# First attention of a fused decoder block: scores as fp32 matmuls in 64x64 blocks, V whole, Y in 64x32 blocks, all engine orders laid anew

## What is computed

```python
q, k, v = split(x @ W_attn)                     # 16 heads of 8 channels
att = q @ k.T / sqrt(8); att = where(causal, att, -inf)
att = polymax(att)      # x*x+1 for x>0, 1-x/100 for -100<=x<=0, else 0; all /1000
x = layernorm(x + (att @ v) @ W_proj)           # first attention
x = layernorm(x + cross_attention(x, ctx, 16 heads of 64))   # softmax; second attention
x = layernorm(x + moe(x))   # 16 experts 128x128, gates from the top 6 of a softmax router
```

## Time and profile before

| | before |
|---|---|
| device time, median of 3 runs | 1042.84 us (1041.07 to 1043.26) |
| the profiled execution | 1043.48 us, its span 1041.4 us |
| PE / PEld busy | 993.9 / 868.0 us |
| DVE / ACT / POOL busy | 978.6 / 762.2 / 395.1 us |
| PE matmul instructions | 16856 |
| granted TensorE clock, mean | 0.986 |

### The profile page before, as it was taken

One profiled execution on the slowest core, in us unless ns is written; L12 is line 12 of the kernel. 1 busy time (PEld: TensorE's weight loads), 2 busy tenths in 40 slices (PEclk: granted clock), 3 DMA queues, 4 the chain that ended last, 5 costly groups with the idle time before them and its releaser, 6 DMA issues.

```text
span 1041.4 us, 44466 instructions
## 1 busy us (share of the span) xinstructions
PE 993.9 (95%) x16856; PEld 868.0 (83%) x16856; DVE 978.6 (94%) x3176; ACT 762.2 (73%) x1606; POOL 395.1 (38%) x681
## 2 busy tenths in 40 slices
PE   5999999999999999999999999999999999999974
PEld 4788888888888888888888888888888888888763
DVE  6779999999999999999999999999999999999766
ACT  5886787777778777778777777877777877776531
POOL 1432344433334434334443333444433444332331
PEclk9999999999999999999999999999999999999987
DMA  5100110000000000010000000000000000010000
GB/s 174 38 23 3 28 28 8 17 25 25 25 25 25 0 25 25 25 25 25 15 10 25 25 25 25 25 1 24 25 25 25 25 20 5 25 37 7 7 2 15
DMA packets 29577, 25.16 MB, mean 24 GB/s; under 512 B 2528, under 2 KB 24544, under 8 KB 29536
## 3 DMA queue, kind: packets, MB, share of 16 engines
q1 hardware_dynamic: 29536, 24.57, 8.5%
HBM read 20.37 MB, written 4.19 MB: 24 GB/s over the span
## 4 chain that ended last, share of the span: by engine, by line
DVE 39%; issue 26%; PE 24%; POOL 4%; ACT 4%; DVEq 2%; DMA 0%; ACTq 0%; POOLq 0%; SPq 0%
PE ps L420 22%; DVE sums L860 15%; DVE allowed L824 4%; DVE ps L831 3%; DVE stats L777 3%; DVE p L805 2%; ACT x L733 2%; POOL rstd L985 2%; DVE p L837 1%; DVE residual L860 1%; DVE left L896 1%; PE ps L571 1%; DVE mv L783 1%; PE ps L548 1%; DVE residual L945 1%
## 5 line engine op out<-in xcount | busy, mean ns | idle before, releaser
L860 DVE SCALAR_TENSOR_TENSOR sums<-ps,gate,sums 128x128 f32<-128x128 f32 x896 | 241.7, 345 | 1.5 <-ACT x L733 1.2
L992 POOL TENSOR_TENSOR p<-p,rowinv 128x1024 f32<-128x1024 f32 x64 | 121.9, 1904 | 36.0 <-DVE rowinv L813 36.0
L982 POOL TENSOR_TENSOR rstd<-mv,ln_eps_tile 128x2 f32<-128x2 f32 x96 | 18.7, 195 | 295.3 <-DVE mv L783 292.0
L420 PE MATMUL ps<-wo_sb,oT 128*128 128x128 f32 x1024 | 122.7, 278 | 2.9 <-issue 0.5
L420 PEld LDWEIGHTS ps<-wo_sb,oT 128*128 128x128 f32 x1024 | 116.7, 192 | 6.7 <-issue 6.2
L733 ACT ACTIVATE x<-residual,shift,rstd 128x128 f32<-128x128 f32 x192 | 83.9, 487 | 39.9 <-POOL shift L987 39.7
L420 PE MATMUL ps<-ex_hi,x2T_hi 128*128 128x512 f32 x256 | 106.7, 417 | 5.3 <-DVE p L805 2.7
L635 ACT ACTIVATE relu<-ps 128x512 f32<-128x512 f32 x128 | 75.9, 596 | 45.2 <-PE ps L420 44.5
L420 PE MATMUL ps<-ex_lo,x2T_hi 128*128 128x512 f32 x256 | 102.8, 402 | 0.0
L420 PE MATMUL ps<-ex_hi,x2T_lo 128*128 128x512 f32 x256 | 102.6, 401 | 0.0
L824 DVE SCALAR_TENSOR_TENSOR allowed<-ps,const 128x512 f32<-128x512 f32 x128 | 87.6, 686 | 8.5 <-ACT relu L635 5.7
(11 more groups left out here) (122 smaller groups left out, 2970.1 us busy)
## 6 DMA issues: line engine op xcount, KB each, us to landing
...
```

The lines of the kernel that those rows point to most:

```text
L420: return pe.matmul(o, l, r, start=start, stop=stop)
L860: done = V.scalar_tensor_tensor(after, ps(f"FF{4 * r + q}")[:, C * e:C * e + C], gate[:, r, 4 * q + e:4 * q + e + 1], before, ALU.mult, AL ...
L992: G.tensor_tensor(weights, weights, rowinv[:, r].unsqueeze(2).broadcast_to([P, H, T]), ALU.mult).then_inc(p2_ready, 1)
```

## The change

The first attention is written anew; the second attention, the experts and the norms keep their instructions.

- **Scores.** `s1` makes 8 fp32 matmuls per tile of 64x64 with N = 512, without a split: per call two sequences (columns of the array) by two halves of the channels (rows of the array). A score bank now holds partitions (sequence of the pair, key) and 512 columns = 8 heads x 64 queries. The keys are copied once whole (`kT`), the queries eight times on ACT, each masked to one head of a half (`qm`). `keys_lo` and `queries_lo` are gone from DVE.
- **V** is 2 matmuls of 128x128, N = 128, moved with one ACT instruction.
- **Y** is 64 matmuls of 64x32, N = 64: per row block, four heads after another accumulate into each of four column groups, for two sequences in two row halves, into two PSUM banks.
- **xT** is loaded once instead of doubled (pieces of 256 bytes).
- **Orders.** All orders and banks are laid anew. Lags now go from +7 (K, Q) over +6 (V, scores), +5 (Y), +4 (PR, X1T, K2), +3 (Q2, V2, S2, PT), +2 (AC, WO), +1 (X2T, LG) to 0 (experts). The steady turns are 1 to NT-8 = 24 (24 turns), with longer written-out parts before and after. `AC0 S2_0 AC1 S2_1` stand behind each other, `WO0` and `WO1` apart.
- **Waits.** Gate step 11 and `weigh0` wait for the previous tile's `FF3` and `FF7` to be emptied, `logits` for the previous `logit_exp`; `s1` and `y` increment `heads_begun` before they start.

```diff
-    ("WO0", "B4", -2), ("WO1", "", -2), ("K", "B1", 1), ("Q", "B5", 1), ("S2_0", "P1", -1),
-    ("Y", "B4", 0), ("V2_3", "B0", -1), ("V2_1", "B7", -1), ("PR", "B6", 0), ("X2T", "B1", -2),
-    ("V2_2", "B4", -1), ("LG", "B2", -2), ("V", "B1", 1), ("S1_0", "B5", 1), ("S1_1", "B0", 1),
-    ("S2_1", "P1", -1), ("K2_0", "B4", 0), ("K2_3", "B7", 0), ("K2_2", "B6", 0), ("X1T", "B1", 0),
...
+    ("FF7", "B1", -1), ("Q2_1", "B5", 3), ("Q2_0", "B7", 3), ("Q2_2", "B2", 3), ("V2_1", "B5", 3),
+    ("AC0", "P3", 2), ("S2_0", "P1", 3), ("AC1", "P2", 2), ("S2_1", "P0", 3), ("V2_3", "B6", 3),
+    ("V2_0", "B7", 3), ("V2_2", "B2", 3), ("S1_0", "B4", 6), ("S1_1", "B5", 6), ("WO0", "B3", 2),
+    ("PR", "B0", 4), ("K2_0", "B1", 4), ("Y", "P3", 5), ("S1_2", "B1", 6), ("S1_3", "B2", 6),
+    ("WO1", "", 2), ("K2_1", "B4", 4), ("X2T", "B6", 1), ("PT0b", "B7", 3), ("PT0a", "B0", 3),
+    ("LG", "B6", 1), ("PT1a", "B3", 3), ("PT1b", "B7", 3), ("V", "B1", 6), ("FF0", "B6", 0),
+    ("FF4", "B4", 0), ("FF5", "B5", 0), ("X1T", "B3", 4), ("FF1", "B1", 0), ("K2_3", "B2", 4),
+    ("FF2", "B0", 0), ("Q2_3", "B4", 4), ("K", "B6", 7), ("Q", "B2", 7), ("FF6", "B7", 0),
...
     "ACT": """
+        mQ2_0@3 mQ2_2@3 mV2_1@3 mAC0@2 norm3@-1 mAC1@2 mV2_3@3 exp0@3 mV2_0@3 mV2_2@3 relu0@6 exp1@3 square0@6 relu1@6 square1@6
+        mK2_0@4 base3@0 relu2@6 mY@5 norm2@1 square2@6 relu3@6 mX2T@1 mPT0b@3 square3@6 mK2_1@4 mPT1a@3 mPT1b@3 norm1@4 mV@6 x1_hi@4
...
-FIRST_TURN, LAST_TURN = 3, NT - 3
+FIRST_TURN, LAST_TURN = 1, NT - 8
...
             def v(tile):
...
+                for r in range(NR):
+                    last = mm(ps("V")[:, C * r:C * r + C], xT[:, P * r:P * r + P], w_attn_sb[:, 2 * C:3 * C])
...
-                    for n, (keys, queries) in enumerate(((kp_hi, qm_hi), (kp_hi, qm_lo), (kp_lo, qm_hi))):
-                        for g, unit in enumerate(units):
...
+                pe.sem_inc(heads_begun, 1)
+                for s in range(2):
+                    for g in range(PARTS):
+                        rows, b = slice(PART * g, PART * g + PART), 2 * r + s
+                        done = mm(ps(f"S1_{PARTS * r + g}")[64 * s:64 * s + 64, :], kT[rows, b], qm[rows, b].rearrange("p v t -> p (v t)"))
...
+                for r in range(NR):
+                    for v in range(COLUMNS // HD):
+                        for g in range(GROUPS):
+                            for s in range(2):
+                                h = COLUMNS // HD * g + v
+                                keys, place = slice(64 * s, 64 * s + 64), VALUE_PAD + COLUMNS * (H * r + h) - HD * v
...
-            def queries_lo(tile):
...
-            def keys_lo(tile, parity):
```

More of the change, by code:

```diff
@@ L24 @@
 HD = C // H
-PARTS = 2
-NV = J // PARTS
-PART = P // PARTS
+PART = 64
+PARTS = P // PART
+NV = PART // HD
+COLUMNS = 32
+GROUPS = P // COLUMNS
+VALUE_PAD = COLUMNS - HD
 DK = 64
@@ L109 @@
[L109 to L112, removed]
+        heads_lo1@0 allow0@0 pieces0@0 allow1@0 pieces1@0 p1_0@0 p1_1@0 allow2@0 pieces2@0 allow3@0 p1_2@0 pieces3@0 p1_3@0
@@ L121 @@
     "SP": """
-        x_rows@-1 context@-1 store@-5 store@-4 store@-3 store@-2 store@-1
+        context@-2 x_rows@-2 context@-1 x_rows@-1 store@-8 store@-7 store@-6 store@-5 store@-4 store@-3 store@-2 store@-1
     """,
     "PE": """
-        WO0@-4 WO1@-4 S2_0@-3 K@-1 Q@-1 Y@-2 V2_3@-3 V2_1@-3 PR@-2 V2_2@-3 X2T@-4 S1_0@-1 S1_1@-1 LG@-4 V@-1 S2_1@-3 K2_3@-2 K2_2@-2
-        X1T@-2 K2_0@-2 K2_1@-2 PT0a@-3 PT0b@-3 Q2_3@-2 Q2_2@-2 Q2_1@-2 FF0@-4 AC0@-3 FF1@-4 FF4@-4 Q2_0@-2 PT1b@-3 PT1a@-3 FF5@-4
@@ L127 @@
-        S1_2@-1 S1_3@-1 FF2@-4 FF6@-4 V2_0@-2 FF7@-4 FF3@-4 AC1@-3 WO0@-3 WO1@-3 V2_3@-2 S2_0@-2 Y@-1 V2_1@-2 PR@-1 V2_2@-2 X2T@-3
-        LG@-3 K2_0@-1 S2_1@-2 K2_3@-1 K2_2@-1 X1T@-1 K2_1@-1 PT0b@-2 PT0a@-2 Q2_1@-1 Q2_3@-1 Q2_2@-1 FF5@-3 FF0@-3 FF4@-3 AC0@-2
-        Q2_0@-1 FF1@-3 PT1a@-2 PT1b@-2 FF6@-3 FF2@-3 FF3@-3 V2_0@-1 V2_1@-1 FF7@-3 AC1@-2 WO0@-2 WO1@-2 S2_0@-1 V2_3@-1 V2_2@-1
-        X2T@-2 LG@-2 S2_1@-1 FF0@-2 PT0a@-1 FF5@-2 PT0b@-1 FF4@-2 FF1@-2 AC0@-1 FF2@-2 FF6@-2 PT1b@-1 PT1a@-1 FF7@-2 AC1@-1 WO0@-1
@@ L131 @@
-        WO1@-1 FF3@-2 X2T@-1 LG@-1 FF1@-1 FF0@-1 FF4@-1 FF5@-1 FF2@-1 FF6@-1 FF7@-1 FF3@-1
+        FF7@-8 Q2_1@-4 Q2_0@-4 Q2_2@-4 PR@-3 AC0@-5 AC1@-5 S2_0@-4 V2_3@-4 V2_1@-4 V2_0@-4 S1_0@-1 S2_1@-4 S1_1@-1 V2_2@-4 WO0@-5
+        X2T@-6 WO1@-5 K2_0@-3 Y@-2 S1_2@-1 S1_3@-1 K2_1@-3 LG@-6 FF5@-7 PT0b@-4 FF0@-7 PT1a@-4 FF4@-7 PT0a@-4 V@-1 X1T@-3 K2_3@-3
+        FF1@-7 PT1b@-4 FF2@-7 Q2_3@-3 FF6@-7 FF3@-7 FF7@-7 K2_2@-3 Q2_1@-3 Q2_0@-3 Q2_2@-3 V2_1@-3 AC0@-4 S2_0@-3 AC1@-4 S2_1@-3
+        V2_3@-3 V2_0@-3 V2_2@-3 WO0@-4 PR@-2 WO1@-4 K2_0@-2 K2_1@-2 Y@-1 K2_3@-2 FF1@-6 FF4@-6 FF5@-6 X2T@-5 PT0b@-3 LG@-5 PT1a@-3
@@ new lines @@
+        FF0@-6 PT1b@-3 PT0a@-3 X1T@-2 FF2@-6 FF6@-6 FF3@-6 Q2_3@-2 Q2_2@-2 Q2_1@-2 K2_2@-2 FF7@-6 Q2_0@-2 V2_1@-2 AC0@-3 S2_0@-2
+        S2_1@-2 AC1@-3 V2_3@-2 V2_0@-2 V2_2@-2 WO0@-3 PR@-1 K2_1@-1 K2_3@-1 K2_0@-1 K2_2@-1 WO1@-3 FF1@-5 PT0a@-2 X2T@-4 PT0b@-2
+        LG@-4 PT1a@-2 FF0@-5 X1T@-1 FF4@-5 PT1b@-2 FF5@-5 Q2_0@-1 FF3@-5 FF2@-5 FF6@-5 Q2_2@-1 Q2_1@-1 Q2_3@-1 AC0@-2 V2_1@-1 FF7@-5
+        V2_3@-1 V2_0@-1 AC1@-2 S2_0@-1 S2_1@-1 FF5@-4 WO0@-2 WO1@-2 FF4@-4 V2_2@-1 X2T@-3 LG@-3 PT0a@-1 FF0@-4 PT0b@-1 FF1@-4 PT1b@-1
@@ L132 @@
+        FF2@-4 FF6@-4 PT1a@-1 FF7@-4 FF3@-4 AC0@-1 AC1@-1 FF1@-3 FF5@-3 WO0@-1 FF4@-3 X2T@-2 FF2@-3 LG@-2 FF0@-3 WO1@-1 FF6@-3 FF7@-3
+        FF3@-3 FF5@-2 FF4@-2 FF2@-2 FF0@-2 FF6@-2 FF1@-2 FF3@-2 X2T@-1 LG@-1 FF7@-2 FF0@-1 FF5@-1 FF6@-1 FF3@-1 FF1@-1 FF4@-1 FF2@-1
+        FF7@-1
     """,
     "ACT": """
-        relu3@-2 mAC1@-4 square2@-2 square3@-2 kK@-1 queries_hi@-1 mY@-2 norm2@-4 exp0@-3 mV2_3@-3 mX2T@-4 mV2_1@-3 relu0@-1 mV2_2@-3
-        mV@-1 relu1@-1 norm1@-2 mK2_3@-2 square0@-1 x1_hi@-2 exp1@-3 mK2_1@-2 mK2_2@-2 logit_exp@-4 square1@-1 mPT0a@-3 mQ2_3@-2
@@ L481, in y @@
             def y(tile):
                 wait_emptied(pe, "V", tile)
[L483 to L492 removed]
+                for unit in range(NR * PARTS):
+                    wait_emptied(pe, f"S1_{unit}", tile)
@@ L596, in do @@
                     if int(job[3:]) % PARTS == PARTS - 1:
-                        s1(tile, int(job[3:]))
+                        s1(tile, int(job[3:]) // PARTS)
                     return
@@ L844, in weigh @@
                 if q == 0:
+                    for job in ("FF3", "FF7"):
+                        wait_emptied(dve, job, tile - 1)
                     dve.wait_ge(gate_steps, GATE_STEPS * (tile + 1))
```

233 lines of the change are left out of this document (114 added, 119 removed), and 6 rows, old and new, of the table JOBS.

## The result

The changed kernel takes 1080.97 us (median of four runs, 1080.37 to 1081.78) beside 1041.95 us before on the same chip: a ratio of 1.0375, with an interval of 1.0357 to 1.0393. It is slower by 39 us, where 22 us less were forecast. The profiled execution has a span of 1080.0 us.

A forecast was written before the change was run, and what follows sets the result against it. The prediction took PE and DVE as a double bound of the steady turn. Head 137, loop 724 and tail 94 + 63.5 gave a span of 1018.5, adjusted by +2.1 and -0.6 to 1020 us (2.2% less); range 1001 to 1045.

The forecast's parts named there:

- The turn: Steady part of the loop: one turn takes 30.15 us, 0.55 less than before, with ends of 29.8 and 31.1.
- The wait for ACT's norm: Steady turn: PE's 0.38 us wait before the transposes of x2 goes, with nothing late in its place.
- bank B1: Steady turn: the tightest new place, where K2_0, Y and scores S1_2 follow each other and ACT moves K2_0 late.
- new waits: Rival: waits at bank B1 or on ACT's squares add 0.3 to 0.6 us per turn, 1029 to 1036 us; chance 0.15.
- PE's sum: Steady turn: PE's changed jobs take 8.40 us instead of 8.63, so its own work falls by 0.2 to 30.1.
- The rule of the start floor: Rival from the Trainium skill: matmul starts at least 25 ns apart, Y 3.2 us, total 1094 us; chance 0.01.
- The head: Written-out list before the loop: 117 us of PE work plus 20 lost (between 10 and 30), 137 us.
- The loop: Steady turns: 24 x 30.15 = 724 us, until 861.
- The tail: After the loop: last second scores at 955 (90 + 4 lost), then 63.5 us, with DVE ending last.
- Little more than half busy: Sign of being right: PE is busy little more than half of the stretch after the last second scores.
- the head doesn't hold: Rival: 40 us lost before the loop instead of 20, or DVE waits in the tail; 1035 to 1045 us, chance 0.08.
- a loop that begins after 150: Sign of being wrong: the steady turns start later than 150 us, where 137 was forecast.

## Why the prediction was wrong

**The turn: right.** 29.96 against 30.15. The wait for ACT's norm is gone, as said, and nothing came in its place: neither bank B1 nor the "new waits" rival shows in any row. DVE's busy share is 281.33/299.60 = 94%, where 92% was to show it right: 28.1 a turn against the 27.8 of the sum. Within PE's sum two terms were off and cancelled in part: Y took 1.42 to the scores' start, not 0.90 + 0.19 = 1.09; the exits to WO were cheaper (scores 1.02 with the exit, not 1.27, from 504.85 to 505.87; the same after Y). That makes +0.33 and -0.50, about the 0.19 by which the turn is shorter than forecast. The transposes of x2 are 29.96 apart, where 30.0 to 30.3 was to show it right.

**The rule of the start floor: it doesn't hold for Y.** The trace shows 1.42 us for Y's 128 records, 11 ns each. By what the Trainium skill says in "TensorE: Matmul & The Clock Gate", section "Wait — 56ns, not 53.3ns?" (about 25 ns from start to start), Y would be an estimated 3.2 us. The measurement decides. But both counts take records, and each fp32 matmul leaves two. By the matmuls that the program writes, Y's 64 start 22 ns apart, just below the floor, and the 32 of a call of second scores, with which the prediction argued, 34 ns apart (1.09/32), which is above it.

**The head: the step that failed.** I priced it as the sum of PE's work, 117 us, and 20 lost: 137. It is 191.8. Both terms were too small. PE is busy 143.4 us, 26 more than priced. The sum itself was sound: at the steady turn's mean distance from start to start, the matmuls recorded in the head would take some 115 us (an estimate), and DVE and ACT were priced at 104 and 117 and are busy 106.7 and 126.6. What it left out is that the granted clock is 0.90 on the mean, where I had priced at full clock, and that jobs which stand alone count their whole latency. And 48 us are idle, not 20. The loss of 23 us in the old head was carried over as a number. The head in steady order shows what it hides: DVE takes over the projections of tiles 0 to 4 at 59.31, 88.42, 117.52, 149.32 and 179.52, so each late partial turn takes 29 to 32 us, as much as a full one, though PE is busy only about 25 of them. That loss comes once for every turn of the fill, and the fill grew from four partial turns to eight. My prediction had the observation ("chains that nothing covers") and didn't count how often it would apply.

What the runs show of the cause: not the laid order (4 us between the two orders tried), not in the main the arithmetic (1 us by the ends, 7 by the time outside the loop), hardly the clock as far as it was tested (at most 3 us net for nearly half of what it lacked from 20 to 80 us), no single link of the ring (0 for V, 4 to 8 for the query copies). The depth it is in so far as 54 to 64 us come with the order that leads by four more turns, and one turn less of lead takes 14 off the steady head (but only 2 off the laid one). That the depth by itself costs this, and 16 us for each turn, is argued, not shown: the order changed in more than its lead, and the run that was to show the price of a turn changed the turn too. What sets the late partial turns at about 30 us, though the experts' work is missing in them, stays open; it was seen only in chains: PE, a copy on ACT, PE again, eight query copies, PE. It wasn't tried apart.

**The loop: right.** 724 forecast, 722.6 measured.

**The tail: right, a little short.** 157.5 forecast, 165.6 measured. The last tile's second scores come 97 us into the list (1011.7, for the kernel before), where 94 was forecast, with PE busy 91.9 of them against 91. What follows takes 68.3 against 63.5. DVE has 54.7 us of work there, inside the 54 to 57 of the sum; the rest is its waiting, more than the 2 us that I had allowed. "Little more than half busy" is a bit low for PE, 45.5 of 68.3 at a granted clock of 0.86.

**The sum.** Head +54.8, loop -1.4, tail +8.1: 61.5, which is the 1080.0 of the span less the forecast 1018.5. So nine tenths of the error lie in one term. The rival "the head doesn't hold" had the right place but about half the size (40 lost instead of 20, at a chance of 0.08, where 75 were lost beside the priced work), and none of my ranges reached a head of 190. I had even written down what it would look like, "a loop that begins after 150".

No version among these beats the kernel before. The turn of 29.96 pays only if the ends stay below 83 us (1042 - 959), and the shortest ends seen with that turn are 118, in the run with one query copy, which leaves work out.
